# Rounded high halves of late row chunks taken from memory by GpSimd's transfers, six pair buffers, tail arrays laid over the scores' columns

## What is computed

```
Sim  = (xn @ w1)[:, None] + (ctx @ w2)[None, :] + (xn * w3) @ ctx.T + b   # 128 x 12544
A    = softmax(Sim, axis=ctx rows);  hq = A @ ctx                         # 128 x 256
Batt = softmax(max(Sim)) ; hc = Batt @ xn
x    = x + concat(xn, hq, xn * hq, xn * hc) @ W_qv + b_qv                 # xn = layernorm(x)
x    = x + linear attention of layernorm(x), 16 heads, rotary positions
x    = x + sigmoid(r) * (relu(k)^2 @ W_v)                                 # gated feed-forward
```

## Time and profile before

| | |
|---|---|
| median of three runs | 116.8 us (116.7, 116.8, 117.56) |
| profiled execution, its device time | 117.75 us |
| profiled execution, span of the trace | 116.0 us |
| granted TensorE clock | 1.00 throughout |
| TensorE busy | 108.5 us (94%) |
| VectorE busy | 95.4 us (82%) |
| ScalarE busy | 80.7 us (70%) |
| GpSimd busy | 29.3 us (25%) |
| read from memory | 29.57 MB |

### The profile page before, as it was taken

How to read it: one execution, slowest core, us unless ns; L and a number is a source line. 1 busy time by engine, 2 the same in 40 slices (tenths; PEclk the granted TensorE clock), 3 DMA queues, 4 the chain that set the end, 5 groups by cost and what they waited for, 6 DMA issues and landing times.

```text
span 116.0 us, 1830 instructions
## 1 busy us (share of the span) xinstructions
PE 108.5 (94%) x578; PEld 86.1 (74%) x578; DVE 95.4 (82%) x152; ACT 80.7 (70%) x169; POOL 29.3 (25%) x42
## 2 busy tenths in 40 slices
PE   5989999999999999799999999799999999898990
PEld 2346858685858587588789898689899899787680
DVE  1539989999999997989999969999999937593342
ACT  5057664889999652999998699989997643302460
POOL 2100000000000074012286258799754000100100
PEclk9999999999999999999999999999999999999999
DMA  3999999999999999989999999720000000000001
GB/s 94 339 386 420 418 421 422 417 421 420 420 421 411 415 414 422 390 304 407 422 399 415 417 425 410 266 100 6 3 3 0 0 6 0 0 0 3 0 6 45
DMA packets 8220, 29.82 MB, mean 257 GB/s; under 512 B 1042, under 2 KB 1298, under 8 KB 8082
## 3 DMA queue, kind: packets, MB, share of 16 engines
q1 hardware_dynamic: 8064, 29.69, 64.3%
q10 hardware_dynamic: 146, 0.01, 0.1%
HBM read 29.57 MB, written 0.13 MB: 256 GB/s over the span
## 4 chain that ended last, share of the span: by engine, by line
PE 80%; DVE 10%; ACT 4%; issue 4%; DVEq 0%; ACTq 0%
PE mixed_ps L962 13%; PE scores_ps L894 11%; PE scores_ps L904 8%; PE scores_ps L916 7%; PE scores_ps L919 7%; PE mixed_ps L964 6%; DVE pair L675 6%; PE scores_ps L933 5%; PE scores_ps L881 4%; DVE turned_low L704 2%; PE scores_ps L1049 2%; ACT neg_scores L489 2%; PE scores_ps L944 2%; PE mixed_ps L1101 1%; PE side_ps L981 1%
## 5 line engine op out<-in xcount | busy, mean ns | idle before, releaser
L675 DVE TENSOR_TENSOR pair<-raw,pair 128x1024 fp32r<-128x1024 f32 (+1 forms) x42 | 51.1, 1229 | 3.7 <-ACT pair L470 3.2
L470 ACT ACTIVATE pair<-raw 128x512 fp32r<-128x512 f32 (+1 forms) x42 | 34.1, 811 | 13.9 <-DMA raw<-keys_dram 9.9
L427 POOL CAST pair<-raw 128x512 fp32r<-128x512 f32 x23 | 22.8, 992 | 57.7 <-DMA raw<-rows_dram 37.7
L962 PE MATMUL mixed_ps<-pair,turned_high 128*128 128x512 f32 x88 | 33.8, 417 | 0.9 <-DVE turned_low L704 0.8
L964 PE MATMUL mixed_ps<-pair,turned_low 128*128 128x256 f32 x88 | 24.8, 282 | 0.0
L962 PEld LDWEIGHTS mixed_ps<-pair,turned_high 128*128 128x128 f32 x88 | 16.6, 188 | 4.6 <-issue 1.5
L697 DVE TENSOR_SCALAR_CACHE_REDUCE neg_scores<-scores_ps,neg_max 128x1024 f32<-128x1024 f32 (+2 forms) x14 | 16.0, 1145 | 1.2 <-PE scores_ps L919 0.5
L964 PEld LDWEIGHTS mixed_ps<-pair,turned_low 128*128 128x128 f32 x88 | 16.7, 190 | 0.0
L704 DVE TENSOR_TENSOR turned_low<-scores_ps,turned_high 128x512 fp32r<-128x512 f32 (+1 forms) x24 | 16.0, 670 | 0.3 <-ACT turned_high L502 0.3
L933 PE MATMUL scores_ps<-ident,neg_scores 128*128 128x128 f32 x98 | 14.7, 273 | 1.0 <-ACT neg_scores L489 1.0
L489 ACT ACTIVATE neg_scores<-neg_scores,neg_max 128x1024 f32<-128x1024 f32 (+2 forms) x15 | 14.3, 956 | 0.8 <-DVE neg_scores L697 0.8
(11 more groups left out here) (189 smaller groups left out, 119.6 us busy)
## 6 DMA issues: line engine op xcount, KB each, us to landing
raw<-keys_dram SPq DMA_DIRECT2D x24, 512.0 KB, 9.5
raw<-rows_dram SPq DMA_DIRECT2D x24, 512.0 KB, 7.6
w<-weights_dram SPq DMA_DIRECT2D x1, 1792.0 KB, 10.6
w<-weights_dram SPq DMA_DIRECT2D x2, 512.0 KB, 11.3
const<-const_dram SPq DMA_DIRECT2D x1, 832.0 KB, 13.6
raw<-keys_last_dram SPq DMA_DIRECT2D x1, 256.0 KB, 9.1
raw<-rows_last_dram SPq DMA_DIRECT2D x1, 256.0 KB, 3.3
x_sb<-x_dram SPq DMA_DIRECT2D x1, 128.0 KB, 2.2
```

What stands on the lines that cost most here:

```text
L427: nc.gpsimd.tensor_copy(out=pair[:, use % PAIR_BUFS, 0, 2 * D:4 * D], in_=raw[:, slot(item), 2 * D:4 * D])\
L470: nc.scalar.activation(pair[:, use % PAIR_BUFS, 0, 0:columns], raw[:, slot(item), 0:columns], ACT.Copy)\
L675: nc.vector.tensor_tensor(out=pair[:, use % PAIR_BUFS, 1, 0:columns], in0=raw[:, slot(item), 0:columns], in1=pair[:, use % PAIR_BUFS, 0, 0 ...
L962: nc.tensor.matmul(mixed_ps[:, :].rearrange("p (h d) -> p h d", h=2), probs_high, both[:, :, t * D:(t + 1) * D], start=(k == EARLY and t = ...
```

## The change

Row chunks 15 to 23 (`is_cast`) get their high half otherwise. GpSimd issues a transfer from the rows in memory straight into the high half of the pair buffer; source is fp32 and destination fp32r, so the transfer rounds. ScalarE and GpSimd make no copy for them. The chunk is still loaded into `raw` as well, since VectorE needs it for the low half; VectorE now waits for that load and for the rounding transfer (`cast_landed`, one semaphore for each buffer). GpSimd's transfer waits for `pair_used`, as its copy did, but not for the load into `raw`. There are six pair buffers in place of four, for keys and rows alike. To make room (a buffer is 8 KB in each partition) eleven arrays of the tail, `attn`, `x2_c`, `x2`, `rstd_diagonal`, `xk_t`, `xr_t`, `k_relu`, `k_act`, `gate`, `mixed_out` and `x3`, lie on columns of `neg_scores`. Their instructions and waits are the same.

```diff
-PAIR_BUFS = 4
+PAIR_BUFS = 6
+CAST_FROM = 15
+    def is_cast(k):
+        return CAST_FROM <= k < FULL
+    def highs_before(use):
+        return use - sum(is_cast(k) and row_use(k) < use for k in range(CHUNKS))
...
-        scratch = neg_scores[:, 0:14 * D].rearrange("p (n d) -> p n d", d=D)
+        scratch = neg_scores[:, 0:23 * D].rearrange("p (n d) -> p n d", d=D)
...
-        attn = sb("attn", [P, DH, D + 1])
-        x2_c = sb("x2_c", [P, D])
+        attn = neg_scores[:, 23 * D:23 * D + DH * (D + 1)].rearrange("p (a d) -> p a d", a=DH)
+        x2_c = scratch[:, 21, :]
...
+        cast_landed = [sem(f"cast_landed{n}") for n in range(PAIR_BUFS)]
...
+        def casts(use):
+            return 16 * sum(is_cast(k) and row_use(k) % PAIR_BUFS == use % PAIR_BUFS and row_use(k) <= use
+                            for k in range(CHUNKS))
...
-                pool.wait_ge(loaded[slot(item)], loads(item))
+                if not is_cast(k):
+                    pool.wait_ge(loaded[slot(item)], loads(item))
                 pool.wait_ge(pair_used, use - PAIR_BUFS + 1)
-                nc.gpsimd.tensor_copy(out=pair[:, use % PAIR_BUFS, 0, 2 * D:4 * D], in_=raw[:, slot(item), 2 * D:4 * D])\
-                    .then_inc(pool_high_done, 1)
+                if is_cast(k):
+                    nc.gpsimd.dma_start(out=pair[:, use % PAIR_BUFS, 0, :], in_=rows_full[k])\
+                        .then_inc(cast_landed[use % PAIR_BUFS], 16)
+                else:
+                    nc.gpsimd.tensor_copy(out=pair[:, use % PAIR_BUFS, 0, 2 * D:4 * D],
+                                          in_=raw[:, slot(item), 2 * D:4 * D]).then_inc(pool_high_done, 1)
...
-                if k + 2 < CHUNKS:
+                if k + 2 < CHUNKS and not is_cast(k + 2):
                     rows_high(k + 2)
...
             def take_low(item, use, columns):
-                dve.wait_ge(high_done, use + 1)
+                if use < KEY_SPLITS or not is_cast(use - KEY_SPLITS + EARLY):
+                    dve.wait_ge(high_done, highs_before(use) + 1)
...
             def rows_low(k):
-                if k < FULL:
+                if is_cast(k):
+                    dve.wait_ge(loaded[slot(CHUNKS + k)], loads(CHUNKS + k))
+                    dve.wait_ge(cast_landed[row_use(k) % PAIR_BUFS], casts(row_use(k)))
+                elif k < FULL:
                     dve.wait_ge(pool_high_done, k - EARLY + 1)
                 take_low(CHUNKS + k, row_use(k), tiles_of(k) * D)
```

More of the change, by code:

```diff
@@ L187, in build @@
         q_rot_t = scratch[:, 13, :].rearrange("p (a l) -> p a l", a=DH)
-        attn = sb("attn", [P, DH, D + 1])
-        x2_c = sb("x2_c", [P, D])
+        attn = neg_scores[:, 23 * D:23 * D + DH * (D + 1)].rearrange("p (a d) -> p a d", a=DH)
+        x2_c = scratch[:, 21, :]
         x2_mean = sb("x2_mean", [P, 1])
[L191 to L200, removed]
+        x2 = scratch[:, 22, :]
+        rstd_diagonal = neg_scores[:, 26 * D:26 * D + P]
+        xk_t = scratch[:, 14, :].rearrange("p (a l) -> p a l", a=DH)
+        xr_t = scratch[:, 15, :].rearrange("p (a l) -> p a l", a=DH)
+        k_relu = scratch[:, 16, :].rearrange("p (a l) -> p a l", a=DH)
+        k_act = scratch[:, 17, :].rearrange("p (a l) -> p a l", a=DH)
+        gate = scratch[:, 18, :]
+        mixed_out = scratch[:, 19, :]
+        x3 = scratch[:, 20, :]
         scores_ps = ps("scores_ps", [P, 3, 2 * CHUNK])
```

## The result

| | before | after |
|---|---|---|
| median | 116.78 us (116.7 to 117.56, 4 runs) | 119.66 us (118.86 to 120.33, 4 runs) |
| ratio | | 1.0229, 95% interval 1.0152 to 1.0305 |
| profiled execution | 117.75 us, span 116.0 | 118.86 us, span 116.9 |

The change made the kernel slower by 2.3%. The forecast was 116.2 us, 0.5% faster. The time lies at the upper end of the range that was given (119.7).

What follows compares the result with a forecast made beforehand. TensorE was taken as the bound, at 1.85 us a chunk, with one gap near 72 us. Closing it (-0.90) and late transfers (+0.30) gave -0.60: profiled 117.75 to 117.15, median 116.2 us, range 115.1 to 119.7.

Steps and rivals of the forecast that it cites:

- the hole: TensorE's late start of mix(12) near 72 us, from ScalarE's wait for a pair buffer; six buffers close it, -0.90 us.
- stretched low halves: Three VectorE low halves at 51 to 57 us, lengthened by collisions with GpSimd copies, 0.94 us in all.
- rival 1: Transfers in time, the full 0.90 us gained, and half of the 0.94 us of collisions: 115.4 us; chance 0.18.
- The allowance of 5.7 us: Rows 15's transfer, released about 68.5 us, must land by 74.2 to keep mix(14) on time; later chunks the same.
- Issue on GpSimd: GpSimd's time to issue one rounding transfer: taken as 1.0 us, between bounds of 0.33 and 1.66.
- Rival 2: VectorE stretches GpSimd's issue of each transfer to 2.2 us, so landings come late: 119.9 us; chance 0.14.
- Landing under load: Rounding transfer's issue, latency and data, sharing the queues by halves with `raw`'s loads: 5.4 us, against 4.2 alone.
- in time by 0.3 us at the worst: Rows 15's rounding transfer, at 5.4 us shared, lands within the 5.7 us allowed.
- The sign that I had set for being wrong: TensorE standing at mix(14) and later for over 1 us in sum; one of three such signs.
- A delay counts once: Late rounding transfers, rows 16 to 18: TensorE's stall also moves later deadlines; cost 0 to 1.2 us, taken as 0.3.
- Rival 3: Rounding transfers move under the needed 283 GB/s, at 208 a chunk is 0.67 us too long: 121.2 us; chance 0.08.
- Sum: Whole kernel: 0 - 0.90 for the closed gap + 0.30 for late transfers = -0.60 us.

Runs made afterwards that it cites:

- six_only: Kernel before with six pair buffers and the moved tail arrays, no rounding transfers; 115.68 us against 117.09, ratio 0.9898, stage 42.46 us.
- no_raw: The change without the loads of rows 15 to 23 into `raw`, for timing only; 116.75 us, ratio 0.9931, stage 43.78 us.
- tail_only: Kernel before with only the tail arrays moved onto the scores' columns, four buffers, no rounding transfers; 117.42 us against 117.09, ratio 1.0066.
- four_bufs: The change with four pair buffers in place of six, rounding transfers kept; 128.08 us, ratio 1.0902 to the kernel before.

## Why the prediction was wrong

- **Which wait made the hole: right.** Four buffers held up ScalarE, ScalarE VectorE, VectorE TensorE. Five buffers already close the hole.
- **Size of that gain: right for the hole, too low as a whole.** I took 0.90 us and kept the 0.94 us of stretched low halves for rival 1, at 0.18, since "a copy still is" released by mix(1). It is, but mix(1) itself comes some tenths later, and the margin was 0.06 us. I had the two rows of it in front of me and did not ask how near the tie was. six_only gains 1.39 us in the stage.
- **The allowance of 5.7 us: right from the release, too long by 0.3 from the issue.** TensorE wanted mix(14) at 74.64, so rows 15 had to land at 72.7. That is 5.7 us after mix(9) ended (67.05) but 5.4 after the issue began (67.36). It landed at 74.3, 1.6 late, and TensorE stood 1.73. (The mix that starts at 70.54 in the earlier trace rows is mix(11), not mix(10) as I wrote; the 68.5 us for the end of mix(9) is right all the same.)
- **Issue on GpSimd: too high.** I took 1.0 us, and it was 0.57. Rival 2 is out: VectorE is in the midst of a low half at six of the nine issues, and these took 0.53 to 0.71 us, the other three 0.57 to 0.60. The Trainium skill (SBUF — State Buffer, "Who interferes with whom") infers just this, that an operation with two inputs from SBUF takes only the read side of the shared pair while descriptors need the write side; the trace agrees, with 0.53 to 0.71 us for all nine.
- **Landing under load: the step that failed.** I wrote "1.0 + 1.9 + 1.26 = 4.2 us alone, 5.4 shared". Shared it is 6.9 to 8.2 for rows 15 to 19. Alone it is 3.8 for the first (no_raw), but 5.7 and 6.4 for the next two, issued 2.1 and 1.9 us apart, which is nearly as fast as GpSimd's transfers move. So the sum lacked two terms: a wait before the halves begin, and the queueing of the nine among themselves. Without SyncE's loads the stage still loses 1.32 of the 2.95 us.

  The 1.9 us was a latency from `x_sb`, the first load into empty queues, and I left it as it was for queues that moved 416 GB/s. The halves fit; that they begin 4 us after the issue was not in the sum. Nor was "in time by 0.3 us at the worst" the worst of my own bounds: with 1.66 us for the issue it would have been 6.1, 0.4 late.

  The row of the loads' landings, median 7.6 us for the same 512 KB, was the nearer one, and would have given 7.6 against 5.7: 1.9 us late at rows 15, which is close to what came, in part by luck: those loads wait behind others of their own queue, which GpSimd's transfer does not.

  The sign that I had set for being wrong, over 1 us of stalls at mix(14) and later, was met with 2.86.

  The Trainium skill (DMA: Bandwidth & Descriptors, "Queues, rings and completion order") says that a memory engine takes turns between its queues; by that alone a new transfer would share at once. The landings of SyncE's loads show turns by halves, but only after 4 us and more.
- **"A delay counts once": nearly right.** Later deadlines did move with the first stall, yet rows 16 was late once more, by 1.13 us, as its landing took 7.8. After two stalls the remaining transfers were hidden.
- **Rival 3 was half right.** GpSimd's transfers move at about 284 GB/s of full share in no_raw, hardly the 283 that the loop needs. Rounding has a part in it (7 to 13% more of the engines' time), but plain ones pile up too, and at rows 15 both land in 6.8 to 6.9 us.
- **Sum.** 2.86 us of stalls against 1.39 gained: 1.5 us in the stage, as measured (1.56). Forecast were 0.3 and 0.9.

## What to carry to other kernels

A transfer put on a path that something waits for must be priced with the landing time that transfers have at that moment, not with an early one in empty queues; rows of the same size at the same place in the trace are the price. Where another queue has many microseconds of loads ahead, move the transfer to after they run out (rows 19 on cost almost nothing here) or leave it out: the gain of this change was all in one or two more buffers, and 0.9898 of the time before is to be had without any rounding transfer. Where two engines block each other and start within a tenth of a microsecond, treat the order as a coin that any small delay turns. And where a stall is long, look at the granted clock before the whole of a loss is put down to the wait: with four buffers it took up to 3.5 us of its own.

## What the runs showed of the hardware

- A rounding transfer (fp32 to fp32r) lands as soon as a plain one from GpSimd, 3.7 against 3.6 us alone and 6.8 against 6.9 under load, but holds the memory engines longer: nine took 14.7 against 13.8 us without the loads and 13.9 against 12.4 beside them, and issued 1.1 to 1.7 us apart they landed 0.1 to 0.6 us later.
- A transfer from GpSimd into full queues had no effect on SyncE's loads for 4 us (landings 1.25 us apart), then both ran at half rate (2.5 us apart). With more queued ahead it waited 6.6 us (an estimate from landings at 62.7 and 2.5 us apart).
- GpSimd's rounding transfers of 512 KB alone in the queues moved 247 GB/s at a share of 0.87, where SyncE's plain ones moved 416 at 1.02; issued 1.7 to 2.1 us apart they landed in 4.4 to 6.4 us, against 3.8 for the first. Plain ones 1.1 to 1.7 us apart landed in 4.6 to 5.2 us, against 3.6 for well spaced ones.
- 4.7 MB of additional transfers, in queues that were full up to 72 us, lengthened nothing in the stage of the rows (42.47 against 42.46 us).
- In the traced execution of tail_only the granted clock was 0.61 in the mean between 108 and 112 us, and 0.50, the level of 1.2 GHz, from 108 to 111; TensorE had been busy 3.65 of the 4.00 us before. In most executions it stayed at 1.00 (2.4 GHz).
- In four_bufs it fell to 0.50 from 79 to 81 us and from 89 to 91 us. Ahead of each fall TensorE had stood still, from 75.7 to 78.5 us and from 85.7 to 87.5 us, and had then begun again. In the trace of the change, with idles of 1.48 and 0.89 us, the clock stayed at 1.00.
